# Layer 1 attention of a two-layer kernel: scores from two float32r parts in 64-row halves of the array, with padding matmuls

## What is computed

```python
q = x @ W_q; k = x @ W_k; v = x @ W_v
latent_kv = (k + v) @ W_down_kv                    # 32 wide
k_rec, v_rec = latent_kv @ W_up_k, latent_kv @ W_up_v
scores = einsum('bhqd,bhkd->bhqk', qh, k_rec) / sqrt(128)
scores = scores * exp(-0.01 * |t_q - t_k|)         # decay by distance
out = softmax(scores) @ v_rec; out = out @ W_o
```

## Time and profile before

| | us |
|---|---|
| median of 3 runs (lowest, highest) | 1563.39 (1562.93, 1563.98) |
| the profiled execution, its time | 1561.7 |
| its span, first to last instruction | 1559.6 |
| mean granted clock over the span | 0.917 |
| busy in the span: PE 86%, DVE 72%, ACT 58%, PEld 48%, POOL 30% | |

### The profile page before, as it was taken

The page is one execution under the profiler, slowest core; times in us unless marked ns, Lnnn a source line. Parts: engine busy times, 40 slices in busy tenths (PEclk is TensorE's granted clock), DMA queues, the critical chain, the costliest instruction groups (busy, mean ns, idle before and its releaser), DMA issues. The chain is left out here.

```text
span 1559.6 us, 23543 instructions
## 1 busy us (share of the span) xinstructions
PE 1334.3 (86%) x7952; PEld 751.4 (48%) x7952; DVE 1128.4 (72%) x1737; ACT 906.1 (58%) x1496; POOL 474.1 (30%) x986
## 2 busy tenths in 40 slices
PE   4298988619999999999754989999999979999998
PEld 1133333407877778777321222222222225777776
DVE  4366674377999999998547766888888243778885
ACT  3288885105555555555330766787887802767774
POOL 3255453003343343343220233223442301212210
PEclk8599999859999999999855898999999968999999
DMA  5524420015666666663347556665563040022110
GB/s 139 107 56 88 80 61 8 3 41 127 151 150 147 151 155 140 157 148 72 123 96 92 72 128 123 102 106 87 88 98 49 15 157 3 26 97 82 61 49 27
DMA packets 71415, 142.57 MB, mean 91 GB/s; under 512 B 11815, under 2 KB 44648, under 8 KB 64392
## 3 DMA queue, kind: packets, MB, share of 16 engines
q1 hardware_dynamic: 70660, 140.62, 41.3%
q10 hardware_dynamic: 648, 0.59, 0.1%
HBM read 124.20 MB, written 16.71 MB: 90 GB/s over the span
## 5 line engine op out<-in xcount | busy, mean ns | idle before, releaser
L1385 DVE CUSTOM_DVE_ANT_0 a_junk<-a_mring,a_COR 128x1024 bf16<-128x1024 f32 x256 | 304.8, 1222 | 90.0 <-PE a_mring L1286 89.8
L1373 ACT ACTIVATE a_PR<-a_ring 128x512 f32<-128x512 f32 x576 | 300.7, 603 | 118.7 <-PE a_ring L1317 118.6
L1260 POOL TENSOR_SCALAR_AFFINE_SELECT a_PR<-a_PR 128x128 f32<-128x128 f32 x512 | 134.6, 293 | 304.0 <-ACT a_PR L1373 303.8
L803 ACT ACTIVATE e_HH<-e_H 128x512 fp32r<-128x512 f32 x184 | 116.4, 633 | 162.5 <-DVE e_H L851 161.8
L1317 PE MATMUL a_ring<-a_QP,a_KP 74*128 74x512 bf16 (+3 forms) x768 | 181.2, 341 | 13.1 <-issue 5.7
L402 DVE TENSOR_SCALAR a_PR<-a_PR,a_lo,a_hi 128x1024 f32<-128x1024 f32 (+1 forms) x160 | 122.1, 774 | 77.1 <-ACT a_PR L376 74.4
L376 ACT ACTIVATE a_PR<-a_ring,a_ng 128x1024 f32<-128x1024 f32 (+1 forms) x160 | 155.0, 1033 | 13.3 <-PE a_ring L305 12.5
L1336 PE MATMUL a_OUT<-a_PR,a_V 128*9 128x512 f32 (+3 forms) x1536 | 154.7, 500 | 0.0
L822 DVE TENSOR_TENSOR e_HL<-e_H,e_HH 128x512 fp32r<-128x512 f32 x138 | 140.3, 1017 | 13.2
L1317 PEld LDWEIGHTS a_ring<-a_QP,a_KP 74*128 74x128 bf16 x768 | 57.9, 99 | 172.4 <-ACT a_PR L1373 119.6
L1676 DVE TENSOR_TENSOR e_HL<-e_GL,e_HH 128x512 fp32r<-128x512 f32 x144 | 109.2, 763 | 37.6 <-ACT e_HH L1644 34.1
(11 more groups left out here) (232 smaller groups left out, 2344.8 us busy)
## 6 DMA issues: line engine op xcount, KB each, us to landing
e_ROUTE<-routing SPq DMA_DIRECT2D x24, 704.0 KB
a_QP<-q_parts SPq DMA_DIRECT2D x72, 192.0 KB
e_RAW<-in_w_chunks SPq DMA_DIRECT2D x46, 192.0 KB, 7.5
a_QM<-q_parts SPq DMA_DIRECT2D x64, 128.0 KB, 5.4
e_GATE<-gates SPq DMA_DIRECT2D x8, 1024.0 KB, 4.7
e_ROUTE<-routing SPq DMA_DIRECT2D x8, 640.0 KB
a_KP<-k_parts SPq DMA_DIRECT2D x24, 192.0 KB
e_ROUTE<-routing SPq DMA_DIRECT2D x8, 576.0 KB
```

Source lines behind the costliest of these rows:

```text
L803: nc.scalar.activation(HH[n % NH][:], HT[n % NH][:], ACT.Copy).then_inc(high_done, 1)
L1260: last = nc.gpsimd.affine_select(out=d, in_=d, compare_op=keep, fill=0.0, base=0, pattern=[[step, P]], channel_multiplier=-step)
L1373: nc.scalar.activation(PR[g % NPR][:, j, :], ring[n % NRING][:], ACT.Exp).then_inc(s_read, 1)
L1385: nc.vector.tensor_tensor_reduce(out=junk[:, i % 2, :], in0=mring[k % 2][:], in1=COR[:, c:c + S], scale=1.0, scalar=-3.0e38, op0=ALU.mult, ...
```

## The change

- **Parts.** q and k are cut into two float32r parts (`high` by an ACT cast, `low` by a DVE subtraction) instead of three bfloat16 parts; second cast, third subtraction and the value matmuls leave `project_l1`. The values are made at the start of `attention_l1`, in the score ring, and copied by ACT, which then also issues 16 DMAs that store batch 0's other heads.
- **Packs.** One pack serves maxima and scores. A head's contraction is 32 product rows and 32 rows for the maxima (2 used, the others zero), 64 in all; heads 0 and 1 of a quad lie in array rows 0 to 63, heads 2 and 3 in rows 64 to 127. POOL sets the constant rows, and clears the query ones for each later half. An iteration is loaded by 8 query and 6 key DMAs, in pieces of 2 KB and 4 KB. The rows of maxima go by four DMAs a half instead of two.
- **Order of PE.** A group becomes twice: one padding matmul (`keep_busy`: bfloat16, 128 rows, 128 x 512, its result overwritten unread), then the pieces of two score units alternating with the pieces of one maximum tile, whose head lies in the other half of the rows (`MAX_ORDER`, `unit_head`). `turn` moves to the front of its group. A tile's 1024 keys are now one head's, in one half of the rows, in 2 or 3 pieces. Ahead of the groups, each of the 22 tiles is followed by 3 padding matmuls, and 24 more come before the first group.

Its core (the masks, the exponentials, the maxima on DVE and `weigh` stay as they are but for names):

```diff
@@ -36,6 +36,7 @@
+PARTS1 = 2
...
-                def values(f):
-
-                    if f:
-                        pe.wait_ge(v_kept, f)
-                    for n in range(FILL):
-                        at = (f * FILL + n) * P
-                        last = nc.tensor.matmul(psV[:, n * VW:(n + 1) * VW], lat[:, at:at + P], WV[:], start=True, stop=True)
-                    last.then_inc(v_ready, 1)
...
-                def second_part(g, w):
-                    act.wait_ge(rest_done, g * NV + w + 1)
-                    nc.scalar.activation(part(g, w, 1), rest[:, w, g % 2], ACT.Copy).then_inc(part2, 1)
+                    nc.scalar.activation(parts[:, w, 0, grp(g)], val[:, w, g % 2], ACT.Copy).then_inc(high_done, 1)
...
+                act.wait_ge(first_stored, 2 * NV * 2 * 16)
+                packs.load_k(act, 0)
...
+                            dve.wait_ge(high_done, g * NV + w)
+                            nc.vector.tensor_tensor(parts[:, w - 1, 1, grp(g)], val[:, w - 1, g % 2], parts[:, w - 1, 0, grp(g)].bitcast(F32),
+                                                    ALU.subtract).then_inc(low_done, 1)
...
+                n = 1
+                for h in range(2):
+                    packs.clear(h, rows_set)
+                    pool.wait_ge(rows_set, n + 2)
+                    packs.set_ones(h, rows_set)
+                    pool.wait_ge(rows_set, n + 4)
+                    n += 4
...
-MROWS = 32
-MAX_ORDER = (0, 2, 1, 3)
+HROWS = 64
+NROWS = 2 * PARTS1 * HD
+MAX_ORDER = (2, 0, 3, 1)
...
+        self.parts = sb("p1_parts", [P, 4, PARTS1, TOK], F32R)
+        self.Q = [sb(f"a1_QP{s}", [P, 2, 2, 2, GW], F32R) for s in range(2)]
+        self.K = [sb(f"a1_KP{s}", [P, 2, 2, S], F32R) for s in range(2)]
...
+        for pair in range(2):
+            heads = slice(q * HQ + pair * 2, q * HQ + pair * 2 + 2)
             for r in range(2):
-                rows = slice(g * MROWS + r * 16, g * MROWS + r * 16 + 16)
-                eng.dma_start(self.Q[s][rows].rearrange("r h a t -> r (h a) t"), self.QS[heads, :, 0:2, :, b * S:(b + 1) * S].rearrange("h a i d t -> (i d) (h a) t"))\
-                    .then_inc(self.q_loaded[s], 16)
+                rows = slice(pair * HROWS + r * 16, pair * HROWS + r * 16 + 16)
+                eng.dma_start(self.Q[s][rows, half].rearrange("r h a t -> r (h a) t").bitcast(F32),
+                              self.QS[heads, :, :, :, tok].rearrange("h a i d t -> (i d) (h a) t")).then_inc(self.q_loaded[s][half], 16)
...
+            for rows, i0, i1 in ((slice(r0, r0 + 16), 0, 2), (slice(r0 + 16, r0 + 24), 1, 2), (slice(r0 + 24, r0 + 32), 0, 1)):
+                eng.dma_start(self.K[s][rows].rearrange("r h a t -> r (h a) t").bitcast(F32),
+                              self.KS[heads, :, i0:i1, :, tok].rearrange("h a i d t -> (i d) (h a) t")).then_inc(self.k_loaded[s], 16)
...
+    def clear(self, h, done):
+
+        for pair in range(2):
+            rows = slice(pair * HROWS + NROWS, (pair + 1) * HROWS)
+            self.nc.gpsimd.memset(self.Q[h // 2 % 2][rows, h % 2].rearrange("r h a t -> r (h a t)").bitcast(F32), 0.0).then_inc(done, 1)
+
+    def set_ones(self, s, done):
+
+        for pair in range(2):
+            rows = slice(pair * HROWS + NROWS, (pair + 1) * HROWS)
+            self.nc.gpsimd.memset(self.K[s][rows].rearrange("r h a t -> r (h a t)").bitcast(F32), 1.0).then_inc(done, 1)
...
+    def unit_head(g, n):
+
+        first = issued(g - 1) if g else LEAD
+        swap = first < issued(g) and max_head(first) < 2
+        return (2, 3, 0, 1)[n] if swap else n
...
-        QP = [sb(f"a1_QP{s}", [PAIRS + 2, 2, HQ, 2, GW], BF16) for s in range(2)]
-        KP = [sb(f"a1_KP{s}", [PAIRS + 2, HQ, 2, S], BF16) for s in range(2)]
...
+                        for pair in range(2):
+                            row = pair * HROWS + NROWS + i
+                            sp.dma_start(QP[s][row:row + 1, h % 2].rearrange("p j a t -> p (j a t)").bitcast(F32),
+                                         MT[pair * NTILE:(pair + 1) * NTILE, i, :].bitcast(F32)).then_inc(m_rows, 16)
...
+                sp.wait_ge(stored[0], STORES * 16)
+                packs.load_q(sp, 2)
+                packs.load_k(sp, 1)
+                packs.load_q(sp, 3)
...
+                    if 1 <= h < NHALF - 3 and T == (1 if half else KB // 2 + 1):
+                        pool.wait_ge(s_read, h * UNITS)
+                        pool.wait_ge(masked, masked_groups(g - 1) * HQ)
+                        clear(h + 3)
...
+                def max_pieces(m):
+
+                    cut = (m // NTILE % 2 * 4 + m % NTILE // HQ + 1) * P
+                    edges = sorted({0, GW, cut, S})
+                    return [(a, b, int(b <= cut)) for a, b in zip(edges, edges[1:])]
...
+                    rows = slice(j // 2 * HROWS, (j // 2 + 1) * HROWS)
+                    if a == 0:
+                        if i == 0:
+                            pe.wait_ge(packs.q_loaded[s][h % 2], (h // 4 + 1) * packs.Q_LOADS)
+                            pe.wait_ge(packs.k_loaded[s], (h // 4 + 1) * packs.K_LOADS)
+                            if h >= 2:
+                                pe.wait_ge(cleared, (h - 1) * 2)
+                        slot_free(k)
+                    last = nc.tensor.matmul(mring[k % 2][:, a:b], QP[s][rows, h % 2, j % 2, var, row * P:(row + 1) * P],
+                                            KP[s][rows, j % 2, var, a:b], start=True, stop=True)
+                    if b == S:
+                        last.then_inc(m_filled, 1)
...
+                    last = nc.tensor.matmul(ring[u % NRING][:, a:b], KP[s][rows, j % 2, var, kb * P:(kb + 1) * P],
+                                            QP[s][rows, h % 2, j % 2, var, a:b], start=True, stop=True)
+                    if b == GW:
+                        last.then_inc(s_filled, 1)
...
+                    tiles = range(issued(g - 1) if g else LEAD, issued(g))
+                    parts_of_unit = list(segments(g % NT, g // NT % 2))
+                    for two in range(2):
+                        u = g * HQ + 2 * two
+                        if u >= NRING:
+                            pe.wait_ge(s_read, u - NRING + 1)
+                        keep_busy(u)
+                        scores = [(n, *piece) for n in (2 * two, 2 * two + 1) for piece in parts_of_unit]
+                        maxima = max_pieces(tiles[two]) if two < len(tiles) else []
+                        for x in range(max(len(scores), len(maxima))):
+                            if x < len(scores):
+                                score_piece(g, *scores[x])
+                            if x < len(maxima):
+                                max_piece(tiles[two], *maxima[x])
...
-                    for m in range(issued(g - 1), issued(g)):
-                        max_tile(m)
...
+                def values(f):
+
+                    if f >= NRING:
+                        pe.wait_ge(v_kept, f - NRING + 1)
...
+                def keep_busy(n):
+
+                    nc.tensor.matmul(ring[n % NRING][:], ID[:], ID[:].unsqueeze(1).to_broadcast([P, GW // P, P]), start=True, stop=True)
...
+                    for piece in max_pieces(m):
+                        max_piece(m, *piece)
+                    if m == 0:
+                        pe.wait_ge(v_kept, NFILL)
+                    for n in range(3):
+                        keep_busy(n)
+                for n in range(24):
+                    keep_busy(n)
...
-                        for j in range(HQ - 1):
-                            scores(g, j)
-                        maxima(g)
-                        scores(g, HQ - 1)
+                        group(g)
...
+                for n in range(STORES):
+                    packs.store(act, n // 8, n % 4, n // 4 % 2, HQ, H, stored[0])
```

More of the change, by code:

```diff
@@ new lines, in __init__, with store @@
+        self.Q = [sb(f"a1_QP{s}", [P, 2, 2, 2, GW], F32R) for s in range(2)]
+        self.K = [sb(f"a1_KP{s}", [P, 2, 2, S], F32R) for s in range(2)]
+        self.q_loaded = [[sem(f"q_loaded{s}{half}") for half in range(2)] for s in range(2)]
+        self.k_loaded = [sem(f"k_loaded{s}") for s in range(2)]
+    def store(self, eng, g, w, i, h0, h1, done):
+        tok = slice(g * GW, (g + 1) * GW)
+        eng.dma_start((self.QS if w < 2 else self.KS)[h0:h1, w % 2, i, :, tok], self.parts[h0 * HD:h1 * HD, w, i, tok].bitcast(F32))\
+            .then_inc(done, 16)
@@ L1107, in attention_l1 @@
+def attention_l1(nc, t, packs, consts, OD):
     NT = KB + 1
@@ L1247, in _, with clear @@
                 store(NHALF - 1)
-                sp.wait_ge(out_stored, NHALF * 16)
+                for half in range(2):
+                    sp.wait_ge(out_stored[half], NIT * 16)
             @block.gpsimd
             def _(pool):
-                for g in range(NGROUP):
-                    T, half = g % NT, g // NT % 2
+                def clear(h):
+                    packs.clear(h, cleared)
```

(20 more changed lines are left out.)

304 lines of the change are left out of this document (112 added, 192 removed).

## The result

The changed kernel takes **1638.0 us**, median of 3 runs (1629.1 to 1645.5): 1.045 times the time before, 95% interval 1.040 to 1.050. The forecast was 1600 with a range of 1543 to 1643, most likely slower: the sign is right, and the measurement lies at the upper end of the range, with a loss of 75 us where 37 were forecast.

The account below looks back on a forecast made before the run. PE's order was taken to set the pace, above a DVE floor of about 2.15 us a group. On the profiled 1561.7, -13 before the first scores and +50 in the groups gave 1598.7, forecast as 1600; range 1543 to 1643.

Parts of the forecast that it names:

- The mechanism: Whole kernel: PE's order sets the pace; first scores come 13 us earlier, groups take 50 us more.
- Projection: Before the first maximum tile: less work on DVE brings that tile at about 798 instead of 826.4, -28 us.
- Ahead of the groups: From first maximum tile to first scores: 22 tiles, turn and 24 paddings take 41 us instead of 25.7, +15.
- Groups: The 144 groups: 3.05 us each plus 8 for the turn, 447 us instead of 397.1, +50.
- The turns: In the groups: at the front and in float32, the turn adds 0.5 x 16 = 8 us.
- where no mask is due: POOL's clears in the groups, 3.6 us a half, were costed at nothing because no masks wait there.
- Sum: Whole kernel: -13 and +50 give +37 on the profiled 1561.7, 1598.7 us.
- The stop before half 2: Early groups: PE's 5.7 us idling there was to go, with 2 MB in 14 DMAs an iteration.
- paddings whose changes are free: Rival, around paddings: changes of array arrangement cost nothing, group 2.72, total 1548 us; chance 0.28.
- halves one after the other: Rival, phases of the groups: array halves don't run abreast in float32r, +115 us, about 1715; chance 0.04.
- The clock fell in the groups: Rival, in the groups: a fifth of them at 1.2 GHz would add 63 us, 1663; chance 0.06.
- The rule of the Trainium skill: Rule against the change, in phases: same-half loads wait for the matmul before, group 3.35, +43 us, 1643; chance 0.05.

Follow-up runs that it names:

- e4: The changed kernel with POOL's clear meant to come one group later; its wait stayed, so the clear did not move; 1628.9 us.
- e11: The changed kernel with only 24 paddings before the groups and 12 before the tiles, a later clear, and key DMAs queued first; 1546.6 us, ratio 0.987.

## Why the prediction was right

**The mechanism held**: PE's order sets the pace, the groups grow, and what the projection saves doesn't pay for it. Step by step:

- *Projection*: forecast first tile 798, measured 805.1. The last part on DVE ends at 789.9 (787.4 forecast), of which 1.1 is a later start. The 6 key DMAs took 0.49 us each to issue, not 0.35, and landed 13.5 us after the last issue, where 7 to 10 were forecast. 7 us too low.
- *Ahead of the groups*: forecast 41, measured 64.0. **This is the term that was mis-sized.** I costed the tiles at full clock with 4 us until it rises, a figure that no row shows, trusting that a PE without gaps gets it. The row I had said 0.50 with PE half busy, and I read the idle half as the whole cause. A PE without gaps wasn't enough: the clock stayed 0.50 to 864.5 with PE never idle. At full clock the term was right: e4's second half has 1.41 to 1.47 us a tile, as the 1.4 forecast. 23 us.
- *Groups*: forecast 447, measured 455.1, of which 454.0 lie between first and last exponential. Groups without a turn took 2.94 to 3.16 from `weigh` to `weigh`, in the mean 2.98, not 3.05: 10 us fewer. The turns cost 0.85 in each odd half and 2.3 in six even ones, 22 us in all, not 8: 14 more, 9 of them from the clears, which I had costed at nothing as "where no mask is due". I looked for what waits behind them on POOL's queue and not for what runs beside them on DVE. Clock dips are another 3.
- *Sum*: 7 + 23 + 8 = 38, from 1598.7 to 1637, against a profiled 1638; the rest lies behind the groups.

That 1638 lies inside the range owes something to how the clock fell: five other kernels with the same work ahead took 44.4 to 54.0 us for it, not 64.0, and the prediction had 41.

The stop before half 2 is gone, as forecast, but fewer DMAs with fewer bytes don't do it alone: without paddings PE stops again, once an iteration. Of the rivals, paddings whose changes are free fell: each change measures 0.11. So did halves one after the other. The clock fell in the groups for 3.4 us twice, not for a fifth of them. The rule of the Trainium skill (TensorE: Matmul & The Clock Gate, Part 3, The mechanism), that a load overlaps running matmuls only where the row groups differ, isn't borne out for halves either: the second unit of a phase uses the rows of the first and starts 0.34 behind it, which is 0.11 for the first load and the 0.23 of the earlier trace rows. Its own load lies at 1022.31 to 1022.49, under the first unit's 1022.20 to 1022.70. The same section names a background weight buffer as a second way to load early, and that fits.

Why is the change slower, though its halves do run side by side? Before, units and tiles of a group took 1.41 (1002.92 to 1004.33 in the earlier trace rows); two phases take 1.32. That is 0.09 won, and the paddings take 0.32 twice: 2.94 instead of 2.39. Without them the ring binds at 2.59. e11's middle halves, 25.0 and 24.4 to 24.6 us, are still longer than the 23.9 of before: the groups without a turn take 2.65 in the mean, before 2.54. The turn's group takes 3.8 in odd and 3.1 to 3.4 in even halves, before 3.6. What e11 gains over the kernel before is the earlier first score (845.6 instead of 852.1) and the early halves, which no longer stop: the first five take 122.5 us instead of 137.7. The later ones give back 11 of these 15: groups 391.4 instead of 395.9.

## What to carry to other kernels

Padding that is to hold the clock is first measured by leaving it out: here the paddings in the groups and behind the tiles held nothing, and cost 56 us and 24 us. In the seven kernels without paddings behind the tiles, the clock rose in an unbroken run of 8 to 24 paddings or within 2 us behind it; that such a run raises it isn't shown, since no kernel is without one. An instruction added to a ring is free where the ring waits and costs its full time in front of the item that the reader needs next; two equal paddings cost 0.03 and 0.32 us a group. And a kernel made faster asks for its loads earlier: when a gain is smaller than the sum says, look for a wait that the slower form had hidden.

## What was not expected of the hardware

- With paddings behind the tiles, the clock ahead of the groups rose at times that the work doesn't explain. With the same paddings, the stretch from first tile to first score took 64.0, 53.7, 44.7, 44.7, 54.0 and 44.4 us in six kernels that do the same there; without them 36.4 to 36.7 in four. Kernels with paddings there spread over 9 to 23 us from run to run, those without over 8 to 14.
- In several runs the clock fell to 0.5 among the groups for 3.4 or 6.8 us, mostly but not only behind a stop of PE.
- DVE's TENSOR_SCALAR on 128x32 took 0.18 us alone, 0.27 beside POOL's masks and 1.76 beside a POOL memset, ending with it. The maxima kept their 1.22 us beside both. SCALAR_TENSOR_TENSOR took 0.17 alone and up to 0.31 beside the masks; it never ran beside a memset.
- Two matmuls on 64 rows each, in different halves of the array, start within 0.01 us and take together what one does, in float32r; before the change only the 32-row groups in bfloat16 showed it.
